# Self-attention of layer 3 in a fused four-layer decoder: half of a unit's heads lose their maximum on VectorE, the other half get it as the bias of ScalarE's exponential

## What is computed

```python
def _L3_attn_ref(x, Wq, bq, Wk, bk, Wv, bv, Wo, bo, rel_emb):
    q = split_heads(lin(x, Wq, bq)); k = ...; v = ...
    rel = rel_emb[r[None, :] - r[:, None] + (MAX_LEN - 1)]
    qk = jnp.einsum('bhld,bhrd->bhlr', q, k) / np.sqrt(HEAD_DIM)
    qk = qk + jnp.einsum('bhld,lrd->bhlr', q, rel)
    att = jax.nn.softmax(qk, axis=-1)
    out = jnp.einsum('bhlr,bhrd->bhld', att, v)
    ...
    return lin(out, Wo, bo)
```

## Time and profile before

| | us |
|---|---|
| median of three runs | 5138.06 |
| the three runs | 5144.56, 5138.06, 5127.23 |
| the profiled execution | 5115.77 |
| its span, first to last instruction | 5114.2 |
| busy in it: PE, DVE, ACT, POOL | 4349.8, 2662.4, 1868.7, 989.0 |
| L3A from max(0) to the end of turned(15), in the four passes | 85.5, 84.4, 81.1, 84.4 |

### The profile page before, as it was taken

How to read it: one execution, slowest core, us unless ns; L and a number is a source line. 1 busy time by engine, 2 the same in 40 slices (tenths; PEclk the granted TensorE clock), 3 DMA queues, 4 the chain that set the end, 5 groups by cost and what they waited for, 6 DMA issues and landing times. The chain is left out here.

```text
span 5114.2 us, 63506 instructions
## 1 busy us (share of the span) xinstructions
PE 4349.8 (85%) x23432; PEld 2336.0 (46%) x23432; DVE 2662.4 (52%) x5937; ACT 1868.7 (37%) x3296; POOL 989.0 (19%) x1124
## 2 busy tenths in 40 slices
PE   6798889889679888988967988898896898889888
PEld 3454444643344444464334444446434454444643
DVE  6556343744655634374465563437446555343744
ACT  3243222436324322243632432225363243222536
POOL 2121110313212211032321211103232121100322
PEclk8898899979789889998978989999897898999989
DMA  2000100000100010000010001000001000100000
GB/s 81 1 3 27 59 6 0 3 18 1 57 1 3 27 59 6 0 3 18 1 57 1 3 27 59 6 0 3 18 2 55 1 3 27 59 6 3 1 18 4
DMA packets 20912, 93.11 MB, mean 18 GB/s; under 512 B 5228, under 2 KB 14444, under 8 KB 17796
## 3 DMA queue, kind: packets, MB, share of 16 engines
q1 hardware_dynamic: 20580, 88.80, 4.6%
HBM read 86.70 MB, written 2.10 MB: 17 GB/s over the span
## 5 line engine op out<-in xcount | busy, mean ns | idle before, releaser
L217 POOL TENSOR_SCALAR rstd_e<-mean_var 128x4 f32<-128x4 f32 x120 | 27.3, 227 | 2413.6 <-DVE mean_var L183 2413.2
L2196 DVE TENSOR_TENSOR arena<-ps,arena 128x512 f32<-128x512 f32 x256 | 176.4, 690 | 466.7 <-ACT arena L2146 466.7
L2146 ACT ACTIVATE arena<-ps 128x512 f32<-128x512 f32 x288 | 171.9, 597 | 605.8 <-PE ps L2094 605.7
L1641 ACT ACTIVATE arena<-ps 77x512 f32<-77x512 f32 x384 | 196.1, 590 | 420.8 <-PE ps L1559 420.8
L2093 PE MATMUL ps<-xT,w_even 128*128 128x512 f32 x576 | 307.9, 617 | 3.1 <-DVE arena L2183 3.1
L2548 PE MATMUL ps<-w_even,w_odd 128*128 128x512 f32 x640 | 304.2, 619 | 2.8 <-issue 2.8
L2100 PE MATMUL ps<-arena,w_even 128*128 128x512 f32 x576 | 295.0, 594 | 6.9 <-DVE arena L2196 4.7
L766 PE MATMUL ps<-xT,w_even 128*128 128x512 f32 (+1 forms) x544 | 269.7, 619 | 0.4
L2094 PE MATMUL ps<-arena,w_even 128*128 128x512 f32 x512 | 265.0, 599 | 0.0
L206 DVE TENSOR_TENSOR y_tok<-ps,x_tok 128x512 f32<-128x512 f32 x72 | 49.4, 686 | 343.1 <-PE ps L704 265.1
L1832 PE MATMUL ps<-arena,w_odd 128*128 128x512 f32 x512 | 220.4, 592 | 0.0
(11 more groups left out here) (440 smaller groups left out, 9340.6 us busy)
## 6 DMA issues: line engine op xcount, KB each, us to landing
w_even<-in_w SPq DMA_DIRECT2D x4, 6916.0 KB, 19.1
w_even<-in_w SPq DMA_DIRECT2D x4, 3313.5 KB, 10.9
w_odd<-in_w SPq DMA_DIRECT2D x4, 2824.5 KB, 9.6
w_odd<-in_w SPq DMA_DIRECT2D x4, 2095.0 KB, 8.5
w_odd<-in_w SPq DMA_DIRECT2D x4, 2048.0 KB, 15.2
x_in<-in_x SPq DMA_DIRECT2D x10, 256.0 KB, 2.9
w_odd<-in_w SPq DMA_DIRECT2D x4, 577.0 KB, 3.3
result<-x_tok SPq DMA_DIRECT2D x8, 256.0 KB, 2.3
```

Source lines behind the costliest of these rows:

```text
L1641: nc.scalar.activation(m["PT"][j % 2][:, c, :], bank(2 + c)[0:KC, :], ACT.Exp, scale=scale)\
L2146: nc.scalar.activation(e_sg[i % 2], bank(i % 2), ACT.Silu).then_inc(e_silu.sem, 1)
L2196: j = nc.vector.tensor_tensor(e_h[i % 2], bank(2 + i % 2), e_sg[i % 2], ALU.mult)
```

## The change

DVE takes the maximum with its sign turned, for all 8 heads as before. It then adds it only to the 512 columns of heads 0 to 3, and signals `c_less_max`. ACT, having waited for that, takes the exponential of these 512 columns in place, and then of heads 4 to 7 in four instructions of 128 columns each, read straight from the unit's second PSUM bank with the turned maximum as the bias column; the last of the four signals `c_exp`. Since ACT now reads the bank, PE's two waits for `c_less_max` become waits for `c_exp`.

```diff
         def act_exp(act, L, u, scale):
             act.wait_ge(c_sub.sem, c_sub[L, u])
             p = CB[L]["P"][u % 3]
-            nc.scalar.activation(p, p, ACT.Exp, scale=scale).then_inc(c_exp.sem, 1)
+            nc.scalar.activation(p[:, 0:4, :], p[:, 0:4, :], ACT.Exp, scale=scale)
+            s = scores_view(L, u)
+            for r in range(4):
+                i = nc.scalar.activation(p[:, 4 + r, :], s[:, 1, r, :], ACT.Exp, scale=scale,
+                                         bias=CB[L]["max"][u % 2][:, 4 + r:5 + r])
+            i.then_inc(c_exp.sem, 1)
...
-            p4 = p.rearrange("p (o r) k -> p o r k", o=2)
-            nc.vector.tensor_reduce(mx.rearrange("p (o r) -> p o r", o=2), s, AX.X, ALU.max)
+            nc.vector.tensor_reduce(mx.rearrange("p (o r) -> p o r", o=2), s, AX.X, ALU.max, negate=True)
             nc.vector.drain()
-            i = nc.vector.tensor_tensor(p4, s, mx.rearrange("p (o r q) -> p o r q", o=2, q=1)
-                                        .to_broadcast([P, 2, 4, m["nk"]]), ALU.subtract)
+            i = nc.vector.tensor_tensor(p[:, 0:4, :], s[:, 0, :, :], bcast(mx[:, 0:4], m["nk"]), ALU.add)
             i.then_inc(c_sub.sem, 1)
...
                 if u >= 2:
-                    pe.wait_ge(c_sub.sem, c_sub[L3A, u - 2])
+                    pe.wait_ge(c_exp.sem, c_exp[L3A, u - 2])
...
                 if i == 16:
-                    pe.wait_ge(c_sub.sem, c_sub[L3A, 15])
+                    pe.wait_ge(c_exp.sem, c_exp[L3A, 15])
                     pe_context_part(pe, L3X, "k")
```

## The result

The changed kernel took 5093.47 us (median of six runs, 5088.09 to 5105.08), beside 5142.59 us for the kernel before (six runs, 5127.23 to 5156.04). The ratio is 0.9918, with a 95% interval of 0.9897 to 0.9938: some 42 us (32 to 53) less, where 16 were forecast. The profiled execution took 5093.23 us, 22.5 less than that of before.

The account below looks back on a forecast made before the run. The POOL loop, 9.03 us per pair of units, was taken as the bound. Gains of 1.5 mid-stage, 0.85 at the start and 1.6 at the end, 3.95 a pass, 16 in four, gave 5138 - 16 = 5122 us; range 5103 to 5141.

Parts of the forecast that it names:

- The loops: Mid-stage, two chains of waits set the pace per pair of units; shortening them saves 1.5 us a pass.
- POOL loop: Chain from scores through max, sub, sums, POOL's product and turn to the next scores; falls from 9.03 to 8.49 us.
- ACT loop: Chain from scores through max, sub, exp, turned, heads and turn; rises from 8.65 to 8.72 us and becomes the bound.
- heads wait for the copy, the turn no longer for POOL: Mid-stage sign on PE that the forecast is right, beside pairs of maxima about 8.7 us apart.
- The small exponentials: ACT's four 128-column exponentials with a bias column, taken to cost 0.26 us each, 1.58 for the whole group.
- the rivals of 0.30 and 0.49: Small exponentials cost 0.30 us each: 5125 us, chance 0.20; or 0.49, not overlapping: 5141 us, chance 0.05.
- The start: First units of the stage: shorter subs bring sums(0), POOL's first product and turn(0) 0.85 us earlier a pass.
- The end: From max(12) to sums(13) DVE never pauses; sub(12), sub(13) and sub(14) each 0.54 shorter, 1.6 us a pass.
- The sum: Whole stage: 1.5 + 0.85 + 1.6 = 3.95 us a pass, 16 us in four.
- the median, which stands 22 us above it, 5138 - 16: Whole program: the median lies 22 us above the profiled execution, giving 5122 us after the change.
- TensorE's clock in the stage moves: Rival: the stage's passes change clock, 5111 us if better (chance 0.18), 5129 if worse (0.09 together with no gain).
- The stage's lead goes on: Behind the stage: the next layer's work stands on ACT right behind turned(15), so the gain passes to it.

Follow-up runs that it names:

- e4: Kernel before with DVE's half and PE's waits of the change; ACT takes heads 4 to 7 in one 512-column exponential without their maximum; ratio 0.9898.
- e8: The changed kernel run again with nothing altered, for a second trace; ratio to the kernel before 0.9912.
- e1: The kernel before with nothing changed, for a second trace; ratio 0.9996.
- e5: Kernel before with the change applied to units 12 to 15 alone; ratio 0.9943.
- e6: Kernel before with the change applied to units 0 to 11 alone; ratio 0.9911.
- e2: Kernel before with only PE's two waits moved from the end of the subtraction to the end of the exponential; ratio 0.9988.
- e9: Kernel before with the maximum of unit 0 taken twice, 1.3 us more on DVE a pass; ratio 1.0029.
- e10: Kernel before with the maximum of unit 0 taken three times, 2.6 us more on DVE a pass; ratio 1.0024.
- e3: Kernel before with the change's split exponentials and PE waits, but DVE still takes the maximum off all 1024 columns; ratio 0.9968.
- e12: The changed kernel with the maximum of unit 0 taken twice, 1.3 us more on DVE a pass; 5104.4 us, ratio to the kernel before 0.9943.
- e7: Kernel before with DVE taking only the maximum and ACT making eight 128-column exponentials from PSUM with the bias; 5075.31 us, ratio 0.9882.

## Why the prediction was right and wrong

**The loops: right.** The POOL loop's 8.49 is e4's 8.50; the ACT loop's 8.72 is the changed kernel's 8.73; heads wait for the copy, the turn no longer for POOL. The small exponentials cost 0.25 (0.26 taken), so the rivals of 0.30 and 0.49 fell.

**The start: right for turn(0), too small for what follows.** turn(0) begins 7.86 after max(0) (952.53 - 944.67) and stood at 8.73, so it is 0.87 earlier, against 0.85. scores(2) begins 3.74 after max(0), as worked out. But it ran at the lower clock here (1.97 and 2.08), so max(2) waited 1.94 us for PE; that was costed at nothing. In e8, at the full clock, scores(2) takes what it took before. What the start saves grows behind turn(0): the second passes of e1 and of the changed kernel lose the same clock up to max(4), 3.4 us, and max(4) begins 17.86 and 16.53 after max(0), which is 1.33 earlier.

**The end: one sub too many.** The row at 1008.05 in the earlier trace rows is max(13), and not max(12) as the prediction has it, since two more of the sixteen maxima follow it. So only sub(13) and sub(14) lie between it and sums(13). Before, and after (max(13) and sums(13)):

```profile
1013.89 1.19 DVE L1334 TENSOR_REDUCE arena<-ps 128x8 f32<-128x1024 f32 x1
...
1018.73 1.21 DVE L1334 TENSOR_REDUCE arena<-ps 128x8 f32<-128x1024 f32 x1
```

```profile
1001.33 1.23 DVE L1338 TENSOR_REDUCE arena<-ps 128x8 f32<-128x1024 f32 x1 [0.19 <-PE ps L2275]
...
1009.54 1.21 DVE L1346 TENSOR_REDUCE arena<-arena 128x8 f32<-128x1024 f32 x1
```

From max(13) to sums(13) is 9.28 before and 8.21 after: 1.07 a pass, two subs at 0.54, where the sum has 1.6. sub(12) stands ahead of max(13), and in e5 its saving doesn't arrive there: the mask columns between the two take 1.62 us instead of 1.09, and max(13) begins 5.13 after max(12) in the first pass, where it was 5.12. Why they take longer was not followed. So the end is worth 4.3 us in four passes and not 6.4, which lies within e5's 2.6 +- 2.2, and e6's 13.3 against 9.4 has the larger start in it.

**The sum: right, with luck in it.** 16 us was forecast, the stage is 16.1 us shorter between the two profiled executions, and 15.6 at equal clock over the runs. The first agreement needs no line: from max(0) to the end of L3X these two executions lost nearly the same clock, 75.3 and 76.3 us in four passes, and that stretch took 693.4 and 678.1 us, 15.3 less. In the second passes of e1 and of the changed kernel sums(13) begins 69.25 and 65.30 after max(0), 3.95 earlier, the forecast of a pass to the hundredth. But in it a start that was too small and an end that was too large cancel, and that is luck.

**From the stage to the program: wrong.** Two steps failed.

The first is "the median, which stands 22 us above it, 5138 - 16": the 22 us were taken as fixed. They went with lost clock. The profiled execution of the earlier trace rows had a mean clock of 0.902, while the unchanged runs have a mean of 0.895: 0.007 x 5138 x 0.684 = 25 us. Only one of 84 later runs of the unchanged kernel was shorter than it. The changed kernel has its median at 5093.47 and its profiled execution at 5093.23, with a clock of 0.902: nothing stands between them any more.

The second is the rival "TensorE's clock in the stage moves". It named the clock, was given 0.18, and was bounded by the stage: 11 us at most, because only the stage's own passes were compared. "The stage's lead goes on" to the next layer was then taken for all that the change does there, and the clock behind the stage was priced at nothing. In the traces the cross-attention behind a shortened stage is never long. The four stretches of L3X stood in the trace of before, 78.4, 73.3, 73.1 and 73.2 with clocks of 0.81 and 0.90, and weren't looked at. In three traces of the unchanged kernel 7 of 12 passes are long, in e2, e9 and e10 all twelve and in e3 two; in the 28 passes of the seven traces with a shortened stage none is.

In us: L3A has 51.2, 64.9 and 75.1 us at the lower clock in the three traces of the unchanged kernel, and 54.6 and 13.7 in the two of the changed one; L3X 72.0, 101.3 and 101.3 against 70.6 and 61.9. The means differ by 30 and 25 us. At half speed 55 us there are 27 of lost clock, of the 44 that the runs show, and 0.684 x 27 = 19 of the 30 us by clock. In these five traces nothing else is shorter: from max(0) to the end of L3X they take 693.4, 708.9 and 713.2 against 678.1 and 662.2 us, 35 less in the mean, and all the rest of the program 4420.8, 4442.2 and 4408.9 against 4413.6 and 4439.3.

**What stays open.** The other 11 us by clock: the five traced executions differ by 32.5 us in the mean, 13 less than the runs do, so most of those us lie in executions of which no trace was kept. Outside the stretch above the traces scatter by some 30 us with and without the change, the cross-attention of layer 1 among them. Nor do these runs show what decides at which level a stage begins; e8 beside the first run of the same program shows only that the idle time ahead of it doesn't. Nor do they show why a stage under 84.5 us is followed by a short L3X. The extra maxima of e9, e10 and e12 cost less at equal clock than the 5 and 10 us that they last. In e10 most of that was taken back within the stage: from max(3) to max(4) is 3.95 us there, and 5.3 to 5.8 in the five passes of the unchanged kernel whose stage has as much time at the lower clock (20.5 us). Those stages take 85.5 to 86.3 us, and e10's 86.4 to 86.5.

## What to carry to other kernels

Read the granted clock not only in the stage that changes but in the stages behind it, and in more than one execution: where the same instructions take two lengths in different passes, a change ahead of them can go with one or the other, and that price belongs in the sum and in the range. To test a gain of a per cent or less, compare at equal clock, and shift the old kernel by a microsecond to see what a shift alone does. Where the rest at equal clock agrees with the sum, check its parts all the same: here two errors cancelled. The loops themselves were read rightly, and pointed on to e7, the whole subtraction on ACT, which is the best of these kernels.

## What the runs showed of the hardware

- One and the same cross-attention took 73, 75, 78.5 or 87.8 us, with 14, 19, 29 or 52 us at 1.2 GHz. The longest was seen in one execution alone, with 1.3 us more work ahead of it on DVE. It took 78.4 us or more behind each of 21 stages of 84.65 us or more, and 75.3 or less behind each of 35 stages of 84.44 or less.
- For the whole unchanged program 1 us of lost clock went with 0.684 us of time, and almost all of the scatter between its runs (5104 to 5168 us) lay on that line.
- Exponentials of 128 columns from PSUM with a bias column began 0.25 us apart, and 0.36 is what the profile gives for each: neighbours overlap by a third.
